# One-hot comparisons in bf16, and four buffers for the first dispatch's normalised rows

## The chip, the cores and the metric

The kernel runs on one core of a Trainium2 chip, as one program. The metric is device time in microseconds (us) from the start to the end of one execution, on that core. An engine's own instruction times are given in us or ns. Engine names are those of the profile: PE is the matrix engine (TensorE), PEld its weight loads, DVE the vector engine, ACT the scalar engine, POOL is GpSimd, SP the queue that issues most DMAs.

## The reference, cut to what matters

The program is a stack of eight residual blocks over `x` of 8 batches x 512 rows x 256 columns: attention and feed-forward by turns. Two of the feed-forward blocks (layers 0 and 2) are mixtures of experts: each of the 4096 rows picks two of eight experts, and the change touches only the code that sorts the rows by expert. For layer 0 the reference is, in essence:

```python
gates = softmax(xf @ gate_w)                  # xf: 4096 rows x 256, normalised
topw, topi = top_k(gates, 2)
topw = topw / sum(topw)
h = einsum('td,edh->teh', xf, w1) + b1        # all experts; only two count
h = gelu(_ln(h, ln1_g, ln1_b))
y = einsum('teh,ehd->ted', h, w2) + b2
out = einsum('ted,te->td', y, combine)        # combine: topw at the chosen two
out = _ln(out + xf, ln_g, ln_b)
```

Layer 2 has the same shape, with a hidden width of 1024, no normalisation inside and the weights from a softmax of the two top logits.

## The kernel before

The stages run one after the other: attention, mixture 0, attention, feed-forward, window attention, mixture 2, attention, feed-forward. A mixture is a `dispatch` stage (L835 to L1104) followed by an expert stage. The expert stage works on 71 tiles (`NTILES`) of 128 rows; each tile belongs to one expert. It fetches its rows with indirect DMAs from the DRAM tensor `rows_in` (`k.zs`), by the row numbers in `k.src`, which the dispatch computes last. No fetch can start before the dispatch has ended.

The dispatch has three parts.

First part, per batch `b` of 512 rows: ACT normalises four tiles into `z[b % Z]` (`normalise`, L958 to L966, the activation is L964), SP stores the buffer to `rows_in` (L903), PE transposes it (`turn`, L920), ACT copies the transposed rows out of PSUM (`copy`, L971), PE computes the eight logits of each row (`logits`, L928). ACT's order is written out by hand: normalise 0 and 1, then for each batch copy `b` and normalise `b + 2`. `Z` is 2, so from `b` = 2 on `normalise(b)` waits until the store of batch `b - 2` has landed (`act.wait_ge(stored[b % 2], ...)`). PE's order is turn 0, and then for each batch turn `b + 1` and logits `b`. Both buffers lie in `work`, a tile whose space later holds the one-hot tiles of the third part. SP's order in the first dispatch is: gate weights, post_b, store 0, the four expert constants (L1575; one is 2048 KB, one 1024 KB, both broadcast to all partitions), and then stores 1 to 7. In the first dispatch POOL also adds `post_b` to each batch of `x` when it has been normalised (L995).

Second part, on DVE alone with three short matmuls of PE between: `select` (L1018 to L1029) picks the two experts of each row, for one half of the tiles after logits 3, for the other after logits 7. Then come prefix sums over tiles and rows (L1037 to L1081), which give each of the 64 row groups (two choices x 32 tiles) its `slot` (place inside a tile, 0 to 127) and its `tile_of` (0 to 70). Every step waits for the one before (`then`).

Third part, eight chunks (`CHUNKS`) of eight row groups (`NJ`), with two buffers each: DVE compares a row of 71 tile numbers with `tile_of` (L1086, 8 x 71 = 568 results per partition, bf16 out), and a row of 128 slot numbers with `slot` (L1088, 8 x 128 = 1024 results, bf16 out). All inputs are float32. One input is a row read again for each group, the other is one element read 71 or 128 times. POOL multiplies the tile one-hot by the group number (L1000), ACT by the row number (L985), and PE multiplies one-hots and names (L951), so that the row numbers appear sorted. DVE's next tile comparison waits for the matmuls two chunks back. After the last chunk DVE computes `k.owner` (L1092 to L1095), and `k.src` and `k.dst` (L1098 to L1104).

Of the kernel before, what the change touches and what calls it, by code (L numbers as in the profile page):

```python
# [16 lines left out]
BF16 = mybir.dt.bfloat16  # L17
I32 = mybir.dt.int32
U32 = mybir.dt.uint32
ALU = mybir.AluOpType  # L20
# [3 lines left out]
P = 128  # L24
NB, SEQ, D = 8, 512, 256
TPB = SEQ // P
# [811 lines left out]
def dispatch(nc, k, L):  # L838
# [12 lines left out]
    with ctx:  # L851
# [4 lines left out]
        Z = 2  # L856
# [11 lines left out]
        z = [work[:, s * (TPB * D):(s + 1) * (TPB * D)] for s in range(Z)]  # L868
# [6 lines left out]
        code = sb(nm + "code", [P, NT])  # L875
        top = [sb(f"{nm}top{j}", [P, NT]) for j in range(TOPK)]
        gap, den = sb(nm + "gap", [P, NT]), sb(nm + "den", [P, NT])
        rank, turn_of, slot, tile_of = (sb(nm + n, [P, TOPK * NT]) for n in ("rank", "turn", "slot", "tile"))
# [11 lines left out]
        stored = [sem(f"{nm}stored{s}") for s in range(2)]  # L890
# [4 lines left out]
        with nc.Block() as block:  # L895
            @block.sync
            def _(sp):
                sp.dma_start(gate[:, :, :], k.a[f"L{L}_gate"]).then_inc(w_in, 16)
                if L == 0:
                    sp.dma_start(post_b[:, :], k.a["L0_ffn_ln_b"].partition_broadcast(P)).then_inc(post_in, 16)  # L900
                for b in range(NB):
                    sp.wait_ge(z_done, b + 1)
                    sp.dma_start(k.zs[P + b * SEQ:P + (b + 1) * SEQ, :].rearrange("(t p) d -> p t d", p=P),  # L903
                                 z[b % Z].rearrange("p (t d) -> p t d", t=TPB)).then_inc(stored[b % 2], 16)
                    if b == 0:
                        load_expert_constants(sp, k, L)
                    k.late(sp, b)
                for s in range(2):
                    sp.wait_ge(stored[s], 16 * NB // 2)
                sp.wait_ge(k.zeroed, 16)  # L910
# [46 lines left out]
            def _(act):  # L957
                def normalise(b):  # L958
                    wait_pos(act, zT_ps, b - Z + 1)
                    if b >= Z:  # L960
                        act.wait_ge(stored[b % 2], 16 * (b // 2))
                    for t in range(TPB):
                        n = b * TPB + t
                        o = act.activation(z[b % Z][:, t * D:(t + 1) * D], k.xt(n), ACT.Identity,  # L964
                                           bias=shift[:, n:n + 1], scale=k.rstd[:, n:n + 1])
                    o.then_inc(z_done, 1)  # L966
# [36 lines left out]
            def _(dve):  # L1003
# [29 lines left out]
                dve.sem_inc(centred, 1)  # L1033
                for h in range(2):
                    select(h)
# [19 lines left out]
                for s in range(2):  # L1055
                    dve.wait_ge(stored[s], 16 * NB // 2)
# [9 lines left out]
                then(dve.scalar_tensor_tensor(slot[:, :], turn_of[:, :], -float(P), rank[:, :], ALU.mult, ALU.add))  # L1066
# [14 lines left out]
                then(dve.tensor_tensor(tile_of[:, :], tile_of[:, :], turn_of[:, :], ALU.add))  # L1081

                for c in range(CHUNKS):
                    s, own = c % 2, slice(c * NJ, (c + 1) * NJ)
                    wait_pos(dve, ids_ps, c - 1)
                    dve.tensor_tensor(at_tile[s][:, :, :], k.cst[:, None, C_J:C_J + NTILES].to_broadcast([P, NJ, NTILES]),  # L1086
                                      tile_of[:, own, None].to_broadcast([P, NJ, NTILES]), ALU.is_equal).then_inc(hot_done, 1)
                    dve.tensor_tensor(at_slot[s][:, :, :], k.cst[:, None, C_I:C_I + P].to_broadcast([P, NJ, P]),  # L1088
                                      slot[:, own, None].to_broadcast([P, NJ, P]), ALU.is_equal).then_inc(slot_done, 1)
# [1448 lines left out]
```

## Time and profile before

| what | us |
|---|---|
| runs of the kernel before | 2286.05, 2288.46, 2291.26 (median 2288.46) |
| profiled execution, device time | 2285.1 |
| its span, first to last instruction | 2283.3 |
| PE busy | 1963.4 (86%) |
| DVE busy | 1310.2 (57%) |
| ACT busy | 941.4 (41%) |
| POOL busy | 593.6 (26%) |
| first dispatch, from DVE's shift (L1032) to `k.dst` (L1104) | 216.7 to 303.6 |
| second dispatch, the same | 1268.6 to 1351.8 |
| mean granted TensorE clock | 0.919 |

The busy shares are means over stages with different limits. Inside the two dispatches the shares are quite other than over the span, so the trace has to be read there, by stretches of time. A duration in the trace covers also the time in which an instruction, already issued, waits for something that is no semaphore.

### The profile page before, as it was taken

To read this page: it belongs to the slowest core of one execution; us is meant where nothing else is said; L and a number is where in the kernel's file an instruction comes from. 1 tells how busy PE (TensorE), PEld (TensorE's weight loads), DVE (VectorE), ACT (ScalarE), POOL (GpSimd) and SP (SyncE) were. 2 spreads that over 40 slices of the span, in tenths; PEclk is the share of its full clock that TensorE was granted. 3 is DMA by queue.
4 is the path that set the end of the run, shared out by engine and by line. 5 is a ranking of instruction groups with operands and counts; after the bars stand their busy time and mean duration, and the time that the engine had idled before them with its cause. 6 is when DMAs were issued, how large, how long until landed. Compare 5 with 4: busy or idle time off the path is not lost. (4 is left out here: it accounts for less than half of the span.)

```text
span 2283.3 us, 37863 instructions
## 1 busy us (share of the span) xinstructions
PE 1963.4 (86%) x11930; PEld 1465.4 (64%) x11931; DVE 1310.2 (57%) x2973; ACT 941.4 (41%) x2050; POOL 593.6 (26%) x582
## 2 busy tenths in 40 slices
PE   6998569999848887999989739999999995998687
PEld 3665536666525553666666729999999983665355
DVE  5885456666558887787655162222222215887987
ACT  3444324444336543333222413333333323553787
POOL 1122246666424431011000032222222221321000
PEclk9999579999959998999989559999999997999899
DMA  7001211111141104000000611111111114100001
GB/s 268 1 1 56 77 49 63 61 64 60 53 162 56 56 1 162 0 1 0 0 15 5 240 33 33 37 34 37 34 37 37 37 31 157 40 20 1 10 28 38
DMA packets 71122, 119.54 MB, mean 52 GB/s; under 512 B 13648, under 2 KB 54736, under 8 KB 67952
## 3 DMA queue, kind: packets, MB, share of 16 engines
q1 hardware_dynamic: 55760, 78.76, 9.9%
q0 software_dynamic: 13680, 37.37, 5.2%
q10 hardware_dynamic: 1584, 2.13, 0.3%
q8 instruction: 58, 0.95, 0.2%
q14 instruction: 40, 0.33, 0.0%
HBM read 86.90 MB, written 31.33 MB: 52 GB/s over the span
## 5 line engine op out<-in xcount | busy, mean ns | idle before, releaser
L1421 ACT ACTIVATE e_hT<-psum,x_bt 128x128 f32<-128x128 f32 x568 | 154.6, 383 | 336.4 <-PE psum L1384 331.7
L1384 PEld LDWEIGHTS psum<-e_xT,e_w 128*128 128x128 f32 x2272 | 268.3, 194 | 8.4 <-ACT e_xT L1414 4.9
L268 POOL TENSOR_TENSOR rstd<-lnt,half 128x4 f32<-128x4 f32 (+1 forms) x72 | 73.3, 1018 | 769.6 <-DVE lnt L262 769.6
L1384 PE MATMUL psum<-e_xT,e_w 128*128 128x128 f32 x2272 | 268.9, 277 | 4.2 <-ACT e_xT L1414 4.2
L1393 PE MATMUL psum<-m_w,e_hT 128*128 x1136 | 256.8, 379 | 0.0
L1393 PEld LDWEIGHTS psum<-m_w,e_hT 128*128 128x128 f32 x1136 | 210.4, 190 | 25.7
L1442 DVE COPY e_w<-m_w 128x2048 f32 x71 | 87.1, 1227 | 234.4 <-PE psum L1384 230.0
L724 DVE TENSOR_REDUCE a_mx<-psum 128x8 f32<-128x512 f32 x192 | 123.2, 684 | 84.0 <-PE psum L515 83.4
L1241 ACT ACTIVATE e_hT<-psum,x_bt,x_gt 128x128 f32<-128x128 f32 x284 | 106.9, 457 | 142.1 <-PE psum L1208 142.1
L1325 POOL DMA_INDIRECT rows_out<-e_y,dst x106 | 106.0, 1000 | 205.7 <-DVE e_y L1452 175.0
L1317 POOL DMA_INDIRECT e_x<-rows_in,src x142 | 142.3, 1002 | 56.8 <-issue 35.2
L640 ACT ACTIVATE a_pT<-psum 128x512 f32<-128x512 f32 x192 | 103.8, 592 | 102.4 <-PE psum L565 102.4
L1218 PE MATMUL psum<-m_w,e_hT 128*128 x568 | 140.4, 390 | 4.0 <-ACT e_hT L1241 3.6
L1199 PE MATMUL psum<-m_w,e_xT 128*128 x284 | 138.2, 609 | 1.4 <-issue 0.6
L1841 PE MATMUL psum<-f_w,f_q 128*128 128x256 f32 x512 | 121.9, 384 | 14.9 <-DVE f_q L1728 14.9
L1841 PEld LDWEIGHTS psum<-f_w,f_q 128*128 128x128 f32 x512 | 97.3, 191 | 55.0 <-issue 30.7
L727 DVE TENSOR_TENSOR a_pr<-psum,a_mx 128x512 f32<-128x512 f32 x192 | 122.9, 682 | 0.7
L1828 PE MATMUL psum<-f_zT,f_w 128*128 128x512 f32 x256 | 121.7, 601 | 0.9 <-DVE f_q L1725 0.9
L1218 PEld LDWEIGHTS psum<-m_w,e_hT 128*128 128x128 f32 x568 | 102.3, 190 | 21.2 <-issue 5.5
L541 PE MATMUL psum<-att_wo,a_oT 128*128 128x256 f32 x384 | 101.4, 387 | 16.5 <-DVE x_res L739 16.5
L487 PE MATMUL psum<-a_zT,att_wq 128*128 128x512 f32 x192 | 103.4, 665 | 7.3 <-ACT a_qT L617 5.2
L244 DVE BATCH_NORM_STATS2 stats<-x_res 128x6 f32<-128x256 f32 (+1 forms) x256 | 98.8, 419 | 12.2 <-PEq L203 8.5
(282 smaller groups left out, 3588.2 us busy)
## 6 DMA issues: line engine op xcount, KB each, us to landing
m_w<-in_L_ffn_w SPq DMA_DIRECT2D x16, 1024.0 KB, 9.3
m_w<-in_L_ffn_w SPq DMA_DIRECT2D x16, 512.0 KB, 12.7
rows_in<-r_work SPq DMA_DIRECT2D x16, 512.0 KB, 5.4
m_w<-rows_out SPq DMA_DIRECT2D x16, 512.0 KB, 5.9
a_ar_g<-rows_out SPq DMA_DIRECT2D x16, 512.0 KB, 5.0
x_res<-in_x SPq DMA_DIRECT2D x8, 512.0 KB, 7.1
m_w<-rows_in SPq DMA_DIRECT2D x8, 512.0 KB, 3.9
out_x<-x_res SPq DMA_DIRECT2D x8, 512.0 KB, 3.0
```

Source lines behind the costliest of these rows:

```text
L724: dve.tensor_reduce(mx[g][:, :], wide[g], AX.X, ALU.max).then_inc(s_max, 1)
L727: dve.tensor_tensor(pr[t % 2][:, g * W:(g + 1) * W].rearrange("p (h l) -> p h l", h=HPC), wide[g], mx[g][:, :, None].to_broadcast([P, HPC, ...
L1199: mm = pe.matmul(h_b[s][:, c * 512:(c + 1) * 512], xT[s][:, kk, :], w1[:, bass.ds(e * (DC * F) + (kk * F + c * 512), 512)], start=(kk == 0 ...
L1218: mm = pe.matmul(y_b[:, 0:D], hT[s][:, f, :], w2[:, bass.ds(e * (FC * D) + f * D, D)], start=(f == 0), stop=(f == FC - 1))
L1241: g = act.activation(hT[s][:, f, :], hT_b[:, f, :], ACT.Gelu, bias=bt[:, col], scale=gt[:, col] if norm else 1.0)
L1317: pool.indirect_dma_start(out=xin[j % 2][:, :], out_offset=None, in_=k.zs[:, :], in_offset=bass.IndirectOffsetOnAxis(ap=k.src[:, j:j + 1], ...
L1325: pool.indirect_dma_start(out=k.ys[:, :], out_offset=bass.IndirectOffsetOnAxis(ap=k.dst[:, j:j + 1], axis=0), in_=y[j % 2][:, :], in_offse ...
L1384: mm = pe.matmul(h_b[s][:, f, :], w1[:, kk, f * P:(f + 1) * P], xT[s][:, kk, :], start=(kk == 0), stop=(kk == DC - 1))
L1393: mm = pe.matmul(y_b[s][:, 0:D], hT[s][:, f, :], k.w2[:, bass.ds(e * (FC * D) + f * D, D)], start=(f == 0), stop=(f == FC - 1))
L1421: g = act.activation(hT[s][:, f, :], h_b[s][:, f, :], ACT.Gelu, bias=bt[:, bass.ds(e * FC + f, 1)])
L1828: mm = pe.matmul(hb[f % HS][:, :], w1[:, kk, f * P:(f + 1) * P], zT[s][:, kk, :], start=(kk == 0), stop=(kk == DC - 1))
L1841: mm = pe.matmul(yb[t % 2][:, 0:D], q[s][:, g, t * P:(t + 1) * P], w2[:, g, :], start=(g == 0), stop=(g == FC - 1))
```

## The change

The two comparisons read bf16 on both sides. Two new tiles, `slots16` and `tiles16`, hold the slot numbers and the tile numbers as bf16; DVE copies them from the float32 constants before `select`. The step that computed `slot` writes bf16 `slot16`, and the step that computed `tile_of` writes its last result to bf16 `tile16`. All these numbers are whole and at most 127, so bf16 holds them exactly. This holds in both dispatches. In the first dispatch alone `Z` is 4: two more buffers of 1024 words each lie beside `work`, there are four semaphores `stored`, and `normalise(b)` waits for the store of batch `b - 4` and for the transpose of batch `b - 4`. The order of ACT, PE and SP stays.

```diff
--- before.py
+++ after.py
@@ -853,7 +853,7 @@
         shift = sb(nm + "shift", [P, NT])
         if L == 0:
             post_b, post_in = sb(nm + "post_b", [P, D]), sem(nm + "post_in")
-        Z = 2
+        Z = 4 if L == 0 else 2
         work = sb(nm + "work", [P, 4 * DC * SEQ])
         taken = [0]
 
@@ -865,7 +865,9 @@
             part = work[:, at:at + words]
             return part.bitcast(BF16) if dtype == BF16 else part
 
-        z = [work[:, s * (TPB * D):(s + 1) * (TPB * D)] for s in range(Z)]
+        z = [work[:, s * (TPB * D):(s + 1) * (TPB * D)] for s in range(2)]
+        if L == 0:
+            z += [sb(f"{nm}z{s}", [P, TPB * D])[:, :] for s in range(2)]
         zT = [work[:, (2 + s) * DC * SEQ:(3 + s) * DC * SEQ].rearrange("p (c q) -> p c q", c=DC) for s in range(2)]
         lgt, eq, rest = (sb(nm + n, [P, NT, E]) for n in ("lgt", "eq", "rest"))
         chosen = k.zero[:, :].rearrange("p (t e) -> p t e", t=NT)
@@ -873,9 +875,11 @@
         old = {c: k.att_w[c][:, :, :].rearrange("p c d -> p (c d)") for c in "qkvo"}
         hot, prod = (old[c].rearrange("p (j t e) -> p j t e", j=TOPK, t=NT) for c in "vo")
         code = sb(nm + "code", [P, NT])
+        slots16, tiles16 = sb(nm + "slots16", [P, P], BF16), sb(nm + "tiles16", [P, NTILES], BF16)
+        slot16, tile16 = (sb(nm + n, [P, TOPK * NT], BF16) for n in ("slot16", "tile16"))
         top = [sb(f"{nm}top{j}", [P, NT]) for j in range(TOPK)]
         gap, den = sb(nm + "gap", [P, NT]), sb(nm + "den", [P, NT])
-        rank, turn_of, slot, tile_of = (sb(nm + n, [P, TOPK * NT]) for n in ("rank", "turn", "slot", "tile"))
+        rank, turn_of, tile_of = (sb(nm + n, [P, TOPK * NT]) for n in ("rank", "turn", "tile"))
         cnt = [sb(f"{nm}cnt{j}", [P, E]) for j in range(3)]
         at_slot = [old[c].bitcast(BF16).rearrange("p (i q) -> p i q", i=NJ) for c in "qk"]
         at_tile = [late(NJ * NTILES, BF16).rearrange("p (i t) -> p i t", i=NJ) for s in range(2)]
@@ -887,7 +891,7 @@
         bank = [ps(f"{nm}b{s}", [P, DC, SEQ]) for s in range(2)]
         lg = [ps(f"{nm}lg{h}", [P, 512]) for h in range(2)]
         pp, idb = ps(nm + "pp", [P, 512]), ps(nm + "ids", [P, 512])
-        stored = [sem(f"{nm}stored{s}") for s in range(2)]
+        stored = [sem(f"{nm}stored{s}") for s in range(Z)]
         (w_in, centred, z_done, zT_ps, zT_copied, lg_ps, lg_read, v, chosen_done, place_ps, gap_done, gap_exp,
          hot_done, slot_done, hi_done, lo_done, ids_ps) = (
             sem(nm + c) for c in ("w_in", "centred", "z_done", "zT_ps", "zT_copied", "lg_ps", "lg_read", "v",
@@ -901,12 +905,12 @@
                 for b in range(NB):
                     sp.wait_ge(z_done, b + 1)
                     sp.dma_start(k.zs[P + b * SEQ:P + (b + 1) * SEQ, :].rearrange("(t p) d -> p t d", p=P),
-                                 z[b % Z].rearrange("p (t d) -> p t d", t=TPB)).then_inc(stored[b % 2], 16)
+                                 z[b % Z].rearrange("p (t d) -> p t d", t=TPB)).then_inc(stored[b % Z], 16)
                     if b == 0:
                         load_expert_constants(sp, k, L)
                     k.late(sp, b)
-                for s in range(2):
-                    sp.wait_ge(stored[s], 16 * NB // 2)
+                for s in range(Z):
+                    sp.wait_ge(stored[s], 16 * NB // Z)
                 sp.wait_ge(k.zeroed, 16)
 
             @block.tensor
@@ -958,7 +962,7 @@
                 def normalise(b):
                     wait_pos(act, zT_ps, b - Z + 1)
                     if b >= Z:
-                        act.wait_ge(stored[b % 2], 16 * (b // 2))
+                        act.wait_ge(stored[b % Z], 16 * (b // Z))
                     for t in range(TPB):
                         n = b * TPB + t
                         o = act.activation(z[b % Z][:, t * D:(t + 1) * D], k.xt(n), ACT.Identity,
@@ -1031,6 +1035,8 @@
 
                 then(dve.scalar_tensor_tensor(shift[:, :], k.mean[:, :], -1.0, k.rstd[:, :], ALU.mult, ALU.mult))
                 dve.sem_inc(centred, 1)
+                then(dve.tensor_copy(slots16[:, :], k.cst[:, C_I:C_I + P]))
+                then(dve.tensor_copy(tiles16[:, :], k.cst[:, C_J:C_J + NTILES]))
                 for h in range(2):
                     select(h)
                 dve.wait_ge(k.zeroed, 16)
@@ -1052,8 +1058,8 @@
                 then(dve.tensor_tensor(k.wt[1][:, :], k.wt[1][:, :], k.wt[0][:, :], ALU.mult))
 
                 dve.wait_ge(place_ps, 1)
-                for s in range(2):
-                    dve.wait_ge(stored[s], 16 * NB // 2)
+                for s in range(Z):
+                    dve.wait_ge(stored[s], 16 * NB // Z)
                 both = lambda t: t[:, :, :, :].rearrange("p j t e -> p j (t e)")
                 each = lambda t: t[:, :, :, :].rearrange("p j t e -> p (j t) e")
                 tiles = cnt[0]
@@ -1063,7 +1069,7 @@
                 then(dve.tensor_scalar(turn_of[:, :], rank[:, :], 1.0 / P, -(0.5 - 0.5 / P), ALU.mult, ALU.add))
                 then(dve.tensor_scalar(turn_of[:, :], turn_of[:, :], MAGIC, None, ALU.add))
                 then(dve.tensor_scalar(turn_of[:, :], turn_of[:, :], MAGIC, None, ALU.subtract))
-                then(dve.scalar_tensor_tensor(slot[:, :], turn_of[:, :], -float(P), rank[:, :], ALU.mult, ALU.add))
+                then(dve.scalar_tensor_tensor(slot16[:, :], turn_of[:, :], -float(P), rank[:, :], ALU.mult, ALU.add))
 
                 then(dve.tensor_scalar(tiles[:, :], tiles[:, :], P - 1.0, 1.0 / P, ALU.add, ALU.mult))
                 then(dve.tensor_scalar(tiles[:, :], tiles[:, :], -(0.5 - 0.5 / P), MAGIC, ALU.add, ALU.add))
@@ -1078,15 +1084,15 @@
                 then(dve.tensor_tensor(start[:, :], end[:, :], tiles[:, :], ALU.subtract))
                 then(dve.tensor_tensor(each(prod), each(hot), start[:, None, :].to_broadcast([P, TOPK * NT, E]), ALU.mult))
                 then(dve.tensor_reduce(tile_of[:, :], each(prod), AX.X, ALU.add))
-                then(dve.tensor_tensor(tile_of[:, :], tile_of[:, :], turn_of[:, :], ALU.add))
+                then(dve.tensor_tensor(tile16[:, :], tile_of[:, :], turn_of[:, :], ALU.add))
 
                 for c in range(CHUNKS):
                     s, own = c % 2, slice(c * NJ, (c + 1) * NJ)
                     wait_pos(dve, ids_ps, c - 1)
-                    dve.tensor_tensor(at_tile[s][:, :, :], k.cst[:, None, C_J:C_J + NTILES].to_broadcast([P, NJ, NTILES]),
-                                      tile_of[:, own, None].to_broadcast([P, NJ, NTILES]), ALU.is_equal).then_inc(hot_done, 1)
-                    dve.tensor_tensor(at_slot[s][:, :, :], k.cst[:, None, C_I:C_I + P].to_broadcast([P, NJ, P]),
-                                      slot[:, own, None].to_broadcast([P, NJ, P]), ALU.is_equal).then_inc(slot_done, 1)
+                    dve.tensor_tensor(at_tile[s][:, :, :], tiles16[:, None, :].to_broadcast([P, NJ, NTILES]),
+                                      tile16[:, own, None].to_broadcast([P, NJ, NTILES]), ALU.is_equal).then_inc(hot_done, 1)
+                    dve.tensor_tensor(at_slot[s][:, :, :], slots16[:, None, :].to_broadcast([P, NJ, P]),
+                                      slot16[:, own, None].to_broadcast([P, NJ, P]), ALU.is_equal).then_inc(slot_done, 1)
 
                 wide = lambda t: t.to_broadcast([1, NTILES, E])
                 then(dve.tensor_tensor(ended[:, :, :], wide(k.cst[0:1, C_J:C_J + NTILES, None]), wide(end[0:1, None, :]),
```

## Rows read from the trace of the kernel before

**Rows 1.** The page: span of the profiled execution.
```profile
span 2283.3 us, 37863 instructions
```
**Rows 2.** Busy time by stretch: dispatch 1 (first four), dispatch 2 (last two).
```profile
core 0: us, PE busy (x) PEld busy (x) DVE busy (x) ACT busy (x) POOL busy (x), PEclk, DMA share, GB/s
...
219.10:228.70 9.60, 9.48 (x56) 8.87 (x56) 0.00 (x0) 5.93 (x10) 6.98 (x3) 0.68 0.98 331
228.70:234.60 5.90, 0.00 (x0) 0.00 (x0) 0.00 (x0) 2.10 (x5) 0.00 (x0) 0.50 0.78 278
234.60:263.30 28.70, 28.65 (x136) 28.55 (x136) 6.98 (x12) 13.73 (x22) 11.78 (x5) 0.50 0.28 92
...
278.30:301.00 22.70, 8.47 (x62) 6.48 (x63) 22.63 (x19) 6.16 (x8) 16.42 (x8) 0.50 0.00 1
...
1280.40:1282.80 2.40, 0.03 (x2) 0.01 (x1) 0.00 (x0) 2.14 (x5) 0.00 (x0) 0.50 1.00 393
1282.80:1311.50 28.70, 28.64 (x136) 28.55 (x136) 3.48 (x12) 14.02 (x22) 0.00 (x0) 0.50 0.88 352
```
**Rows 3.** Timeline around batch 3: start, duration, engine, line; idle before and its releaser.
```profile
225.87 2.80 PE L928 MATMUL psum<-r_gate,r_work 128*128 128x8 f32 x16
...
232.50 2.07 ACT L964 ACTIVATE r_work<-x_res,r_shift,rstd 128x256 f32<-128x256 f32 x4 [6.70 <-DMA rows_in<-r_work]
...
234.62 1.97 PE L920 MATMUL psum<-cst,r_work 128*128 128x128 f32 x8 [5.95 <-ACT r_work L964]
...
239.66 1.95 PE L920 MATMUL psum<-cst,r_work 128*128 128x128 f32 x8
```
**Rows 4.** DMA issues, 221.5 to 223 us: KB each, us from issue to landing.
```profile
x_b<-in_L_ffn_b SPq DMA_DIRECT2D x1, 2048.0 KB, 9.9
rows_in<-r_work SPq DMA_DIRECT2D x1, 512.0 KB, 10.4
```
**Rows 5.** Busy time in two single microseconds: PEclk is the seventh column from the left.
```profile
225.00:226.00 1.00, 1.00 (x10) 0.95 (x10) 0.00 (x0) 0.80 (x1) 1.00 (x2) 1.00 1.05 422
...
227.00:228.00 1.00, 1.00 (x6) 1.00 (x6) 0.00 (x0) 0.00 (x0) 0.70 (x1) 0.50 1.12 442
```
**Rows 6.** Timeline of the chunk loop, dispatch 1: its start, one period, its end.
```profile
278.35 0.75 DVE L1086 TENSOR_TENSOR r_work<-cst,r_tile 128x568 bf16<-128x568 f32 x1
...
280.16 1.68 DVE L1086 TENSOR_TENSOR r_work<-cst,r_tile 128x568 bf16<-128x568 f32 x1
...
281.76 1.21 DVE L1088 TENSOR_TENSOR att_wk<-cst,r_slot 128x1024 bf16<-128x1024 f32 x1
...
281.92 2.05 POOL L1000 TENSOR_TENSOR r_work<-r_work,cst 128x568 bf16<-128x568 bf16 x1 [0.68 <-DVE r_work L1086]
282.89 1.67 DVE L1086 TENSOR_TENSOR r_work<-cst,r_tile 128x568 bf16<-128x568 f32 x1
...
299.29 1.67 DVE L1092 TENSOR_TENSOR r_work<-cst,r_cnt 1x568 f32<-1x568 f32 x1
```
**Rows 7.** Groups by line and shape, DVE: count, busy us, mean ns.
```profile
L1442 DVE COPY e_w<-m_w 128x2048 f32 x71 | 87.1, 1227 | 234.4 <-PE psum L1384 230.0 <-issue 3.0 <-PEq L895 1.4
L1725 DVE SCALAR_TENSOR_TENSOR f_q<-f_u,f_c,psum 128x512 f32<-128x512 f32 x64 | 47.5, 742 | 0.0
L757 DVE SCALAR_TENSOR_TENSOR delta<-a_part,cst,delta 128x512 bf16<-128x512 bf16 x2 | 1.5, 751 | 0.1
```
**Rows 8.** POOL beside DVE outside the dispatches: two timeline rows, one group by line.
```profile
1010.12 0.69 DVE L1720 TENSOR_TENSOR f_u<-f_u,f_near 128x512 f32<-128x512 f32 x1
...
1010.42 2.60 POOL L1655 TENSOR_TENSOR x_res<-x_res,f_b 128x1024 f32 x1
...
L438 POOL TENSOR_TENSOR x_res<-x_res,att_bo 128x1024 f32<-128x1024 f32 x24 | 56.7, 2363 | 1.2 <-ACT a_z L604 1.2
```
**Rows 9.** Timeline: DVE's first step after the logits; PE's first after the dispatch.
```profile
244.85 0.29 DVE L1018 COPY r_lgt<-psum 128x128 f32<-128x128 f32 x1 [27.96 <-PE psum L928]
...
309.62 0.66 PE L1190 MATMUL psum<-cst,e_x 128*128 128x128 f32 x2 [8.08 <-DMA e_x<-rows_in,src]
```

## The prediction

> **What bounds the kernel now.** I read the page first, then busy time by stretches inside the two dispatches, then the timeline of those stretches. The profiled execution has a span of 2283.3 us and a device time of 2285.1 us, so 1.8 us lie outside the span [rows 1]. The dispatches take some 87 and 83 us of it. They stand between two barriers: PE's first matmul of the experts waits for rows that are fetched by numbers which the dispatch computes last [rows 9], and no other stage runs beside it. So whatever shortens the chain inside a dispatch shortens the whole time by as much, and nothing outside a dispatch is touched.
>
> The chain inside has three limits in turn, and the reader is to look at which engine's column fills each stretch [rows 2].
>
> In the first part it is PE: 28.65 of 28.70 us busy from 234.6 to 263.3. Before it, from 228.7 to 234.6, PE does nothing for 5.90 us. The timeline says why [rows 3]: turn 3 waited 5.95 us for ACT's normalise 3, and this waited 6.70 us for a DMA. The DMA is the store of batch 1, issued at 222.03 behind the expert constants; it took 10.4 us to land where the constant of 2048 KB ahead of it took 9.9 [rows 4].
>
> In the second part it is DVE alone, step after step.
>
> In the third part DVE is busy 22.63 of 22.70 us [rows 2], but that figure misleads. One period is from 280.16 to 282.89, 2.73 us [rows 6]. The tile comparison takes 0.75 us when it runs first (278.35) and 1.68 in the loop: issued at 280.16 it ends at 281.84, and POOL's multiplication of the same chunk had been running. In the next period POOL ends at 281.92 + 2.05 = 283.97, and the comparison that was issued at 282.89 ends at 282.89 + 1.67 = 284.56, 0.59 us later. So the tile comparison stands still until POOL is through, and then runs for about 0.6 us. POOL in turn starts 0.08 us after the comparison's end. The period is POOL 2.05 + comparison 0.60 + 0.08 = 2.73. The slot comparison (1.21 us) is not a term of this sum, unless POOL stands still for it, which is the question below.
>
> **Part 1: four buffers in the first dispatch.** Removed is the wait of normalise 3 for store 1. Followed step by step with the measured durations: ACT ends normalise 2 at about 224.2, copy 1 (1.0 us) at 225.2, normalise 3 (2.07) at 227.3. PE ends logits 1 at 225.87 + 2.80 = 228.67 [rows 3], so turn 3 then waits for PE itself and starts at about 228.7 in place of 234.62. This is the whole 5.9 us gap [rows 2].
>
> What is late next? Normalise 4 waits for store 0, long landed. Normalise 5 waits for store 1, which lands at 222.03 + 10.4 = 232.4 [rows 4]. PE needs normalise 5 only for turn 5. A turn and its logits take 239.66 - 234.62 = 5.04 us [rows 3], so turn 5 is due at 228.7 + 10.1 = 238.8 and normalise 5, 2.07 us long, could start as late as 236.7. The cover is 4.3 us. Stores 2 and 3 are now issued sooner, beside store 1; in the kernel before such a store had 512 KB, and at the 331 GB/s of that stretch [rows 2] the two are 1.05 MB or 3.2 us of traffic, so even if all of it got ahead of store 1 the cover holds by 1.1 us. Normalise 6 and 7 wait for stores 2 and 3, and are due 5 and 10 us later still. From turn 3 on PE was gapless before and stays so; everything to the end of logits 7 moves 5.9 us forward.
>
> TensorE's clock could change this. It was at its upper level (1.00, 2.4 GHz) at 225 and at its lower (0.50, 1.2 GHz) from 227 on, while PE was busy throughout [rows 5]. After that it stayed at 0.50 through 28.7 us without a gap, in both dispatches [rows 2]. Since turn 3 falls after the drop in the new order too, I take 0.50 for the same 136 matmuls, and 28.7 us again.
>
> Added in this part are two waits on DVE ahead of the rank computation and two on SP. No row prices a wait whose semaphore is already up. Bounded from below by nothing, from above by the 0.1 us or so between dependent DVE steps, they cost 0 to 0.2 us; I take 0.1. SP's lie beside DVE's 40 us chain. The added copies of constants are hidden: DVE sits idle for 27.96 us before its first step after the logits [rows 9], and would still for 22; the two copies are each no longer than the 0.29 us of that 128-column copy. In the second dispatch the same idle time covers them. Without that cover they would cost 0.6 us each time.
>
> Sum of part 1: -5.9 + 0.1 = -5.8 us.
>
> **Part 2: comparisons in bf16.** The count of elements and the access pattern stay. One input has single elements repeated 71 or 128 times in the innermost dimension. Nothing in the trace is a two-tensor DVE operation in bf16 with such an input, so I bound it. The nearest row is a two-tensor operation with 512 bf16 elements in and out: 751 ns, against 742 ns for the same kind of instruction in float32 [rows 7]. Its bf16 gives nothing. The other end is the float32 copy with one source, 2048 elements in 1.227 us [rows 7], that is two elements per 1.2 ns: DVE can take two at a time, and if a comparison in bf16 could, it would halve. The first row is nearer, for it has two tensor sources as the comparison has. Cost of part 2 taken: 0 for all 32 comparisons. The steps that now write bf16 `slot16` and `tile16` have 64 elements and stay as long.
>
> The Trainium skill has two rules here. VectorE: DVE Perf Modes, section on the perf-mode tier table, says that a bf16 tensor_tensor between SBUF tiles runs at twice the rate of float32; by that alone the change would gain what rival A gives. Vector Engine (DVE) Microarchitecture Reference, section 5.1, says that the doubled mode wants a step of one in every operand, and reports that with one element read again and again as one source of a two-source operation it ran at single rate. By that the sum is the -5.8 us above. No run here shows either yet.
>
> **Forecast.** 2285.1 - 5.8 = 2279.3 us for a profiled execution like this one. The profiled execution lay 3.4 us below the median of the runs, so against the median: 2288.5 - 5.8 = 2282.7 us, 0.25% faster.
>
> **The rivals.**
>
> A. The comparisons halve. From 1.21 us for 1024 and 0.75 for 568 elements [rows 6] one element costs 1.01 ns and the rest is 0.18 us. Halved, the slot comparison takes 0.69 and the running part of the tile comparison 0.60 - 0.29 = 0.31. What that brings depends on whether POOL stands still for the slot comparison. For it: in the feed-forward stage a POOL addition of 1024 elements took 2.60 us where 2.363 is the mean, and a two-source DVE operation that began before it ended 0.39 us after POOL's start [rows 8]. The loop has the same order: slot comparison at 281.76, POOL at 281.92. And 568 elements at POOL's rate (2.36 us for 1024) would be 1.3 us, not 2.05. So POOL probably starts its work when the slot comparison ends (282.97) and takes 1.00 from there. Then the period falls by 0.52 from the slot comparison and 0.29 from the tile comparison, 0.81. Per dispatch: seven periods 5.7, the first comparison 0.3, the last slot comparison 0.5 (what follows it, at 299.29, stays float32): 6.5, twice 13.0. Time: 2282.7 - 13.0 = 2269.7. If POOL needs its 2.05 us anyway, only the tile comparison counts: 16 x 0.29 = 4.6, and 2278.1. Against all of A: the bf16 row of 751 ns.
>
> B. The gap is filled but the gain is lost, because store 1 comes late for normalise 5 as well, or ACT's normalise 3 finds another holder of its buffer. This needs store 1 to land after 236.7 + 5.9 us. Time 2288.5, no change. The 4.3 us of cover speak against it, and that the DMA engines have room after 234.6, where their share is 0.28 [rows 2].
>
> C. Slower: repeated bf16 elements cost DVE two cycles each in place of one. The place is the chunk loop, all 16 chunks. The slot comparison grows by 1024 x 1.01 ns = 1.03 us, and POOL stands still for it; the tile comparison grows by 0.57. The period grows by 1.60, sixteen times 25.6 us: 2282.7 + 25.6 = 2308.3. It decides from 0.36 us per chunk on (5.8 / 16), where the gain of part 1 is eaten, and shows as slower by over 0.2% from 0.65 us per chunk on. Against it: bf16 at step one cost 9 ns more in 742 [rows 7]. For it: only that no row has bf16 with repeated elements.
>
> **How the numbers follow.** Forecast 0.78, A 0.14 (0.10 with POOL released, 0.04 without), B 0.05, C 0.03. The forecast's own range is -5 to -6.5 us, with the two medians' own scatter of about 3 us (the three runs spread over 5.2): 2279 to 2287. To reach 8 in 10 I take in B above and A's weaker form below: 2277 to 2289. A's stronger form and C stay outside, 0.13 together. What a measurement of this kernel can tell from no change is about 0.2%, 4.6 us. The forecast's 5.8 is just above that: of its 0.78 I give 0.53 to faster by over 0.2% and 0.25 to within. With A on the one side, B within and C slower: faster 0.67, same 0.30, slower 0.03.
>
> **What would show it right or wrong.** In the profile after: turn 3 of the first dispatch (L920) starts at 228.7 with no idle time before it, and no ACT normalise waits longer than 1 us for a store; logits 7 end at about 257.4. The second dispatch's first part stays as it is, its 2.40 us gap [rows 2] too. L1086 and L1088 keep 0.75 / 1.67 and 1.21 us, and L1000 keeps 2.05; a slot comparison of 0.7 us would be rival A, and L1000 then tells by 1.5 or 2.05 us which form. A slot comparison above 1.5 us is C. The clock in 234 to 257 at 0.50; were it at 1.00 for part of it, I would be wrong on the fast side.

## The result and the profile after

The changed kernel took 2274.85 us (median of 6 runs, 2272.96 to 2278.99), the kernel before, measured beside it, 2287.26 (6 runs, 2281.55 to 2291.26). The ratio is 0.9949, with a 95% interval of 0.9933 to 0.9965: 11.7 us faster, 8 to 15 by the interval. Forecast were 5.8 us and 2282.7 us, with a range of 2277 to 2289. The time lies below the range. A second comparison of the same two kernels (run `again` below) gave 0.9967, 0.9956 to 0.9978, so 7.5 us, 5 to 10. The intervals overlap from 8 to 10 us. All ratios here leave out slow executions, of which there were two, both of the run `z3` (2321.13 and 2717.28 us).

The page's first line, and then the busy time by stretch (width, busy time and count of PE, PEld, DVE, ACT, POOL, then PEclk, DMA share, GB/s). The first two stretches are the first part of dispatch 1, the third its chunk loop.

```profile
span 2273.2 us, 37869 instructions
```

```profile
216.80:225.90 9.10, 8.99 (x57) 8.62 (x58) 0.00 (x0) 9.01 (x16) 7.22 (x4) 0.69 0.98 316
225.90:254.40 28.50, 28.50 (x137) 28.40 (x136) 7.55 (x12) 12.66 (x21) 11.46 (x5) 0.50 0.46 161
269.40:291.20 21.80, 7.89 (x56) 5.89 (x56) 21.77 (x18) 6.15 (x8) 16.14 (x8) 0.50 0.00 1
```

The 5.90 us in which PE did nothing [rows 2] are gone: the 136 matmuls follow the first 56 at once, and take 28.5 us at the lower clock, where the kernel before took 28.65. The timeline shows the batches (start, duration, instruction, and in brackets the idle time before):

```profile
219.75 2.06 ACT L968 ACTIVATE r_z<-x_res,r_shift,rstd 128x256 f32<-128x256 f32 x4
...
222.30 1.07 PE L924 MATMUL psum<-cst,r_z 128*128 128x128 f32 x8
...
223.20 2.71 PE L932 MATMUL psum<-r_gate,r_work 128*128 128x8 f32 x16
...
225.77 1.95 PE L924 MATMUL psum<-cst,r_z 128*128 128x128 f32 x8
...
232.41 2.07 ACT L968 ACTIVATE r_work<-x_res,r_shift,rstd 128x256 f32<-128x256 f32 x4 [3.63 <-DMA rows_in<-r_work]
...
235.79 1.95 PE L924 MATMUL psum<-cst,r_work 128*128 128x128 f32 x8
```

Turn 3 (225.77) has no idle time before it; it comes 11.36 us after the dispatch's first DVE step at 214.41, where the kernel before had it at 234.62 - 216.70 = 17.92 [rows 3]. ACT's wait did not vanish, it moved two batches on: normalise 5 waits 3.63 us for store 1. Normalise 5 ends at 234.48 and turn 5 starts without idle time at 235.79. Store 1 now took longer, from issue to landing:

```profile
rows_in<-r_work SPq DMA_DIRECT2D x1, 512.0 KB, 12.6
```

against 10.4 us [rows 4]. The chunk loop did not change at all. First one period of it, as in rows 6, and then the two comparisons by shape over both dispatches (count, busy us, mean ns):

```profile
272.87 1.21 DVE L1094 TENSOR_TENSOR att_wk<-r_slots,r_slot 128x1024 bf16<-128x1024 bf16 x1
...
273.03 2.05 POOL L1004 TENSOR_TENSOR r_work<-r_work,cst 128x568 bf16<-128x568 bf16 x1 [0.68 <-DVE r_work L1092]
274.00 1.68 DVE L1092 TENSOR_TENSOR r_work<-r_tiles,r_tile 128x568 bf16<-128x568 bf16 x1
```

```profile
L1092 DVE TENSOR_TENSOR r_work<-r_tiles,r_tile 128x568 bf16<-128x568 bf16 x16 | 24.9, 1559 | 0.1
L1094 DVE TENSOR_TENSOR att_wq<-r_slots,r_slot 128x1024 bf16<-128x1024 bf16 x8 | 9.7, 1213 | 0.0
```

Inputs in bf16 on both sides, and 1.21 us as in float32 [rows 6].

Where do the 10.1 us between the two profiled spans lie? The table cuts each span at the start of the first DVE step of a dispatch (shift) and at the start of its last (`k.dst`). "Its loop" is part of dispatch 1: from the start of the first comparison to the start of the step behind the last one. The table has all profiled executions, one of each kernel; the experiments are explained below. "Logits 0" is the duration of the first batch's 16 logit matmuls on PE, which tells the clock: 1.85 to 2.04 where it rose to the upper level, 3.42 at the lower.

| kernel | to dispatch 1 | dispatch 1 | its loop | between | dispatch 2 | rest | span | logits 0 |
|---|---|---|---|---|---|---|---|---|
| before | 216.7 | 86.7 | 20.9 | 965.2 | 82.9 | 931.8 | 2283.3 | 2.04 |
| null | 216.1 | 87.3 | 20.9 | 960.5 | 82.8 | 932.2 | 2278.9 | 1.85 |
| bf16 | 215.0 | 87.8 | 20.9 | 963.6 | 82.9 | 927.1 | 2276.4 | 1.87 |
| after | 214.4 | 80.1 | 20.9 | 964.4 | 83.1 | 931.2 | 2273.2 | 1.85 |
| again | 218.6 | 83.2 | 20.9 | 963.4 | 83.3 | 932.0 | 2280.5 | 3.42 |
| z4 | 218.7 | 80.1 | 20.9 | 961.3 | 82.8 | 931.4 | 2274.3 | 1.95 |
| z3 | 218.7 | 83.2 | 20.9 | 963.6 | 82.8 | 928.1 | 2276.4 | 3.42 |
| const_late | 215.7 | 83.2 | 20.9 | 965.1 | 80.4 | 931.4 | 2275.7 | 3.42 |
| slot_step | 218.2 | 75.8 | 16.7 | 961.7 | 78.8 | 927.8 | 2262.3 | 1.85 |
| both_step | 214.9 | 78.7 | 16.2 | 963.2 | 78.0 | 933.5 | 2268.3 | 3.42 |
| names_step | 214.7 | 79.9 | 16.6 | 965.8 | 79.4 | 932.3 | 2271.9 | 3.42 |
| best | 215.3 | 75.6 | 16.2 | 962.1 | 75.6 | 928.6 | 2257.2 | 1.89 |
| best2 | 215.7 | 75.8 | 16.7 | 962.1 | 76.3 | 931.3 | 2261.2 | 1.98 |
| best3 | 219.1 | 79.8 | 16.6 | 963.5 | 76.8 | 931.6 | 2270.9 | 3.42 |

From before to after: 2.3 us ahead of dispatch 1, 6.6 in it, 0.8 between, -0.2 in dispatch 2, 0.6 in the rest. Only the 6.6 are in code that the change touches.

### The profile page after: what moved, and what is told of

The parts are those of the page before. It is cut to its first block and busy times, and to the rows that moved or that the text cites. A ratio compares the mean times of both kernels' runs of the same rounds, so it can differ in the third digit from the quotient of the medians.

```text
span 2273.2 us, 37869 instructions
## 1 busy us (share of the span) xinstructions
PE 1962.6 (86%) x11930; PEld 1464.5 (64%) x11931; DVE 1311.3 (58%) x2977; ACT 941.6 (41%) x2050; POOL 592.4 (26%) x582
## 5 line engine op out<-in xcount | busy, mean ns | idle before, releaser
L541 PE MATMUL psum<-att_wo,a_oT 128*128 128x256 f32 x384 | 100.9, 385 | 16.4 <-DVE x_res L739 16.4
```

## The experiments

Two theories were open. **Theory S** (scatter): the change gives some 6.6 us, all in dispatch 1, and the rest of the 11.7 is scatter of stretches that no edit touches. **Theory H** (hidden effect): something systematic outside that stretch gives another 5 us. The first, second, third and fourth run below (`again`, `z4`, `bf16`, `null`) are to tell them apart. Runs measured together share their runs of the kernel before: its median was 2284.61 us beside these four, 2284.85 beside `const_late`, `slot_step`, `both_step` and `best`, and 2283.91 beside `z3`, `names_step`, `best2` and `best3`. A gain in us is the ratio times that median.

### again: the change once more

> The changed kernel once more. Theory S (scatter): its first dispatch gives 6.6 us, and the other 5 us of the 11.7 us that were measured are scatter of the stretches that no edit touches, so this time it comes out between 5 and 9 us below the kernel before. Theory H (hidden effect): something systematic outside the first dispatch gives another 5 us; then it comes out 10 us or more below again.

Measured: 2275.72 us (8 runs, 2274.01 to 2282.27), ratio 0.9967 (0.9956 to 0.9978), 7.5 us. That is the middle of the 5 to 9 us of theory S. Its profile showed something that had not been expected: dispatch 1 took 83.2 us, not 80.1, without a gap on PE and without a wait of ACT for a store. Its first logits:

```profile
224.77 3.42 PE L932 MATMUL psum<-r_gate,r_work 128*128 128x8 f32 x16
```

The same instructions took 1.85 us in the profile of after. The granted clock over eight microseconds from the start of PE's work (PEclk is third from the right), first `again`, then `after`:

```profile
221.00:225.00 4.00, 3.91 (x18) 3.54 (x19) 0.00 (x0) 3.91 (x8) 2.83 (x2) 0.50 0.90 269
225.00:229.00 4.00, 4.00 (x20) 4.00 (x21) 0.00 (x0) 3.84 (x7) 4.00 (x2) 0.50 1.04 383
```

```profile
217.00:221.00 4.00, 3.91 (x21) 3.54 (x20) 0.00 (x0) 3.91 (x8) 2.32 (x2) 0.56 0.96 294
221.00:225.00 4.00, 4.00 (x34) 4.00 (x34) 0.00 (x0) 4.00 (x8) 4.00 (x3) 0.87 1.00 321
```

In one execution the clock rises to its upper level (2.4 GHz) for a few microseconds, in the other it stays at the lower (1.2 GHz), with the same work before and under it. Why is not shown: PE had stood 6.33 us before this work in `again` and 6.32 in `after`.

### z4: the four buffers alone

```diff
-        Z = 2
+        Z = 4 if L == 0 else 2
...
-        stored = [sem(f"{nm}stored{s}") for s in range(2)]
+        stored = [sem(f"{nm}stored{s}") for s in range(Z)]
```

The comparisons keep their float32 inputs.

> Only the four buffers of the first dispatch, comparisons in float32 as before. Theory S: 5.5 to 7 us below the kernel before, within 2 us of the whole change. Theory H, if the hidden part belongs to the buffers: 10 to 13 us below. If it belongs to bf16: 5.5 to 7 us below, and the whole change 5 us faster than this.

Measured: 2275.18 us, ratio 0.9967 (0.9953 to 0.9980), 7.5 us. This equals the whole change in `again`. It is 0.5 us more than theory S expected, with an interval of 4.6 to 10.7 us. Dispatch 1 takes 80.1 us.

### bf16: the comparisons alone

```diff
-                                      slot[:, own, None].to_broadcast([P, NJ, P]), ALU.is_equal)
+                                      slot16[:, own, None].to_broadcast([P, NJ, P]), ALU.is_equal)
```

> Only the bf16 comparisons, two buffers as before. Theory S: no difference, within 2 us of the kernel before; both comparison lines keep 1.21 and 0.75 or 1.67 us. Theory H, if the hidden part belongs to bf16: 5 us below the kernel before.

Measured: 2283.28 us, ratio 0.9996 (0.9988 to 1.0005), 0.9 us with an interval over zero. The loop keeps 20.9 us (20.94 in either profile). The bf16 half of the change does nothing that can be told from zero.

### null: the kernel before, a second time

> The kernel before, unchanged, built and loaded a second time. Theory S: its median can differ from that of the first by 2 to 4 us, by loading alone, and its early stretch (the first 56 us, where transfers land) differs most. Theory H: within 1 us of the kernel before.

Measured: 2283.39 us, ratio 0.9997 (0.9987 to 1.0007). So two builds of one kernel agree within 1.2 us when their medians come from 12 and 28 runs, and no 2 to 4 us by loading were seen. Here theory H had expected the right thing and theory S had not. Single executions scatter much more: the profiled ones of before and null differ by 4.4 us in span, 4.7 of it in the stretch between the dispatches. So the scatter is there, but it is from execution to execution, and largest between the dispatches and not in the early stretch. Theory H stays unlikely for another reason: `z4` and `again` both gave 7.5 us. The upper ends of their intervals, 10.7 and 10.0 us, just reach the 10 us that it needs, so it is not ruled out.

### const_late: the same gap closed from the other side

```diff
-                    if b == 0:
+                    if b == NB - 1:
                         load_expert_constants(sp, k, L)
```

> The kernel before with one move: SP issues the expert constants after store 7 in place of after store 0, in both dispatches; two buffers, float32 comparisons. If the queue of constants ahead of store 1 is the cause of the gap, the stores land in about 3 to 4 us, PE's 5.95 us gap in the first dispatch closes without any new buffer, and the time falls by 5.5 to 7 us, like the four buffers; in the second dispatch the weight loads are still ahead of the stores, so at most 1 to 2 us of its 2.4 us gap go. If the cause were the buffers themselves (two are too few even for undisturbed stores), the gap stays at 2 us or more.

Measured: 2274.50 us, ratio 0.9955 (0.9942 to 0.9968), 10.3 us. The point lies above that of the four buffers, but the intervals overlap. With two buffers as before, PE has no gap in dispatch 1 (83.2 us; the clock stayed at its lower level in this execution), and in dispatch 2 the stage shrank from 82.9 to 80.4 us, the whole gap of 2.40 us [rows 2]. Normalise 3 of the first dispatch and turn 3 of the second:

```profile
224.47 2.07 ACT L964 ACTIVATE r_work<-x_res,r_shift,rstd 128x256 f32<-128x256 f32 x4
...
1275.59 1.97 PE L920 MATMUL psum<-cst,r_work 128*128 128x128 f32 x8
```

No idle time stands before either. A lower clock makes PE later and could hide a gap in dispatch 1, but normalise 3 ended at 226.54, 10.9 us after the dispatch's first step at 215.68, and turn 3 of `after` started 11.36 us after it with the clock risen early. So no gap would be left there either (an estimate from the two profiles). The stores landed in 2.9 us (the median of eight), less than the 3 to 4 us expected. So two buffers are enough once the stores are not held up; the 3 MB of constants ahead of store 1 were what held it, and the 1 MB of them in dispatch 2 as well.

### z3: is a third buffer enough?

Against z4; the waits for the stores are counted to fit.

```diff
-        Z = 4 if L == 0 else 2
+        Z = 3 if L == 0 else 2
```

> Three buffers in the first dispatch in place of four, float32 comparisons. By the reasoning on what is late next: normalise 4 now waits for store 1, which lands some 18 us after the dispatch's first step, so turn 4 starts near 20.5 us after it where PE would be ready at 16.4: a gap of about 4 us remains and the gain over two buffers is about 2 to 3 us in place of 6.6. The rival: any third buffer is enough, and it equals the four.

Measured: 2279.84 us (the median of all eleven; 2278.99 without the two that the ratio leaves out), ratio 0.9984 (0.9975 to 0.9993), 3.7 us. That is half of the four buffers' gain and a little over the 2 to 3 us expected. Its interval and those of `again` (from 0.9956 to 0.9978) and `z4` (from 0.9953 to 0.9980) touch, so that three buffers give less than four is likely and not certain. Its profiled execution is one at the lower clock. ACT's normalise 4 waited there for store 1:

```profile
235.44 2.07 ACT L966 ACTIVATE r_work<-x_res,r_shift,rstd 128x256 f32<-128x256 f32 x4 [4.24 <-DMA rows_in<-r_work]
...
238.22 1.95 PE L922 MATMUL psum<-cst,r_work 128*128 128x128 f32 x8
```

Turn 4 has no idle time before it, so this wait cost PE nothing. With the clock risen early turn 4 would be due 16.4 us after the dispatch's first step (in `after` it started at 230.78) and would find normalise 4 ended 18.8 us after it: an estimated gap of 2.4 us. No profile shows that case.

### slot_step: the slot comparison with a step of one in all operands

The diffs of this and the next two runs are cut to the lines that change a layout or how it is read. This one is against the changed kernel and the next two each against the run before it; declarations and the waits for the spread-out constants are left out, in both_step also the turned tile comparison and ACT's line.

```diff
-        at_slot = [... .rearrange("p (i q) -> p i q", i=NJ) for c in "qk"]
+        at_slot = [... .rearrange("p (q i) -> p q i", i=NJ) for c in "qk"]
-                        mm = pe.matmul(idb[:, 0:2 * NTILES], at_slot[s][:, i, :],
+                        mm = pe.matmul(idb[:, 0:2 * NTILES], at_slot[s][:, :, i],
+                act.activation(slots16[:, :, :], k.cst[:, C_I:C_I + P, None].to_broadcast([P, P, NJ]), ACT.Copy)
-                    dve.tensor_tensor(at_slot[s], slots16[:, None, :].to_broadcast([P, NJ, P]),
-                                      slot16[:, own, None].to_broadcast([P, NJ, P]), ALU.is_equal)
+                    dve.tensor_tensor(at_slot[s], slots16[:, :, :],
+                                      slot16[:, None, own].to_broadcast([P, P, NJ]), ALU.is_equal)
```

> The changed kernel, but the slot comparison's result and both its inputs have the row group innermost (a step of one in all three; the constant is spread out once by ACT); the tile comparison stays with a repeated element. If the repeated element keeps bf16 at single rate, the slot comparison falls from 1.21 to about 0.7 us. If then POOL's multiplication had been standing still for it, POOL's 2.05 us fall to about 1.5 and the time by 0.52 us for each of 16 chunks, 8 us below the changed kernel. If POOL needs 2.05 us by itself, the time stays. If bf16 at a step of one is no faster either, both durations stay.

Measured: 2269.67 us, ratio 0.9935 (0.9920 to 0.9949). One period of its loop:

```profile
276.12 0.68 DVE L1100 TENSOR_TENSOR att_wk<-r_work,r_slot 128x1024 bf16<-128x1024 bf16 x1
...
276.27 1.52 POOL L1010 TENSOR_TENSOR r_work<-r_work,cst 128x568 bf16<-128x568 bf16 x1 [0.68 <-DVE r_work L1098]
276.85 1.55 DVE L1098 TENSOR_TENSOR r_work<-r_tiles,r_tile 128x568 bf16<-128x568 bf16 x1
```

The slot comparison fell by 0.53 us and POOL's multiplication, of which nothing was edited, by 0.53 as well. The loop fell from 20.94 to 16.67 us in either dispatch, 8.5 together, where 8 were expected; by the ratios, 0.9935 against 0.9967, it is 7.3 us. This is the price that rival A put on the slot comparison (0.52 us a chunk), got by the layout and the type together and not by the type alone; float32 in the new layout was not run.

### both_step: the tile comparison too

```diff
-        at_tile = [late(NJ * NTILES, BF16).rearrange("p (i t) -> p i t", i=NJ) for s in range(2)]
+        at_tile = [late(NJ * NTILES, BF16).rearrange("p (t i) -> p t i", i=NJ) for s in range(2)]
-                    pool.tensor_tensor(names[s][:, :, 0, :], at_tile[s][:, :, :], hi, ALU.mult)
+                    pool.tensor_tensor(names[s][:, :, 0, :], at_tile[s].rearrange("p t i -> p i t"), hi, ALU.mult)
```

> As the last one, the tile comparison too with the row group innermost; POOL and ACT then read its result with a step of eight elements. If pairing works for both, the tile comparison runs for about 0.3 us in place of 0.6 after POOL ends, and the time is 4 to 5 us below that of the last kernel, some 12 us below the changed kernel. If POOL or ACT are slowed by the stepped read, POOL's line shows it and eats this.

Measured: 2271.13 us, ratio 0.9938 (0.9924 to 0.9952): nothing gained on slot_step, where 4 to 5 us were expected. ACT reads its result in the same steps as POOL. The groups by line and shape:

```profile
L1012 POOL TENSOR_TENSOR r_work<-r_work,cst 128x568 bf16<-128x568 bf16 x16 | 28.6, 1785 | 91.1 <-DVE r_work L1099 91.1
L997 ACT ACTIVATE r_work<-r_work,cst 128x568 bf16<-128x568 bf16 x16 | 21.6, 1351 | 23.4 <-DVE r_work L1099 23.4
```

The comparison itself now takes 0.45 us when it runs first, against 0.75. But POOL, reading in steps of eight, takes 1.79 us in place of 1.52, ACT 1.35 in place of 0.77. The period is 2.18 us against 2.20: what the comparison gained went to POOL's 0.27 us more. The expectation had named this as what would eat the gain.

### names_step: POOL and ACT in steps of one, PE in steps of eight

```diff
-        names = [... .rearrange("p (i a t) -> p i a t", i=NJ, a=2) for s in range(2)]
+        names = [... .rearrange("p (a t i) -> p a t i", i=NJ, a=2) for s in range(2)]
-                                       names[s][:, i, :, :].rearrange("p a t -> p (a t)"),
+                                       names[s][:, :, :, i].rearrange("p a t -> p (a t)"),
```

> As both comparisons with the row group innermost, and now the names too, so that POOL and ACT read and write in steps of one and only PE's moving operand is read in steps of eight elements. If the stepped read was what took POOL from 1.52 to 1.79 us, it returns to about 1.5 and the period falls from 2.18 to about 1.9 us: 4 us below that kernel. If PE's matmul is slowed by its own stepped read, its 0.33 us grows, and from 0.24 us per matmul more on PE would set the period.

Measured: 2272.77 us, ratio 0.9948 (0.9935 to 0.9961). The 4 us expected below both_step did not come. PE became the bound:

```profile
275.09 2.24 PE L957 MATMUL psum<-r_work,att_wq 128*128 128x142 bf16 x8 [8.24 <-POOL r_work L1012]
...
277.38 0.46 DVE L1099 TENSOR_TENSOR r_work<-r_work,r_tile 128x568 bf16<-128x568 bf16 x1 [1.42 <-PE psum L957]
```

Eight matmuls took 2.24 us where both_step had 1.17 and the kernel before 1.13, and the tile comparison stood 1.42 us until the matmuls of two chunks back were through. POOL took 1.66 us, not the 1.5 expected, with a step of one in what it reads and writes; its group numbers were read in another order too, and why it stayed slower is open. Reading PE's stationary operand in the same steps (slot_step) had cost it nothing to speak of: 1.16 us for eight.

### best, best2, best3: put together

Each adds the late constants (the edit of const_late) to one of the last three kernels: best to both_step, best2 to slot_step, best3 to names_step.

> The last kernel, with the expert constants issued after store 7. If the causes add up: the first dispatch has no gap and no dependence on when store 1 lands, the second loses up to 1 to 2 us of its gap: 1 to 3 us below the last kernel, 20 us below the kernel before.

> Slot comparison with the row group innermost, four buffers in the first dispatch, and the expert constants after store 7: 8.5 us from the comparison, 7 to 8 from the first dispatch, 1 to 3 from the second: 2284.8 - 18 = 2267.

> The names-innermost kernel with the expert constants after store 7: 4 us below the last one if POOL returns to 1.5 us, so about 2263, 22 us below the kernel before.

Measured: best 2266.87 us, ratio 0.9925 (0.9910 to 0.9940); best2 2265.18 us, 0.9924 (0.9911 to 0.9937); best3 2266.70 us, 0.9932 (0.9919 to 0.9945). The intervals overlap, so which of the three is first is not settled. Best2 is the simplest and is 17.4 us faster than the kernel before, some 10 us faster than the changed kernel; 18 had been expected of it, and 20 of best, which gave 17.1. Dispatch 2 falls from 83.1 (after) to 76.3 and 75.6 us. Best3 was expected at 2263 and its loop, 16.6 us, was bound by PE as in names_step.

## Why the prediction was right or wrong

**Part 2, the comparisons: right, by a row that was partly luck.** They were costed at nothing, by the 751 ns row [rows 7]; they gave 0.9 us with an interval over zero. The slot comparison stayed at 1.21 us. But the 751 ns row is a scalar_tensor_tensor with a step of one in its tensors, and it was read as saying that bf16 gives two-source operations nothing. slot_step shows that a bf16 comparison with a step of one does gain: 1024 elements in 0.68 us. What kept the changed kernel's comparisons slow is the repeated element, and no row of before had one in bf16. Vector Engine (DVE) Microarchitecture Reference, section 5.1, in the Trainium skill had said that a source with one element read again and again keeps single rate; the trace agrees with 1.21 us for 1024 bf16 elements, and with 0.68 us once the same comparison had a step of one. The rule of the Trainium skill in VectorE: DVE Perf Modes, section on the perf-mode tier table, that bf16 doubles the rate of a tensor_tensor, held nearly for the slot comparison in slot_step (0.68 us, with the fixed part of the instruction in it) and not in the changed kernel (1.21 us). The sub-step of rival A that was called probable, that POOL stands still for the slot comparison, is shown by POOL's 2.05 going to 1.52 us. The Trainium skill's page SBUF — State Buffer, section on who interferes with whom, says that a DVE instruction with two SBUF inputs and a GpSimd instruction that reads SBUF exclude each other. The trace agrees in both orders: POOL's multiplication took 2.05 us behind a comparison of 1.21 us and 1.52 behind one of 0.68, and DVE's tile comparison took 1.55 to 1.68 us behind POOL's multiplication and 0.75 when it ran first. Rival B's late store came (the 3.63 us below) and cost PE nothing. Rival C had no part: a repeated bf16 element costs what a repeated float32 element costs.

**Part 1, the mechanism: right.** The gap closed, turn 3 lost its idle time, nothing new appeared on PE, the clock in the later stretch stayed at 0.50, the second dispatch kept its gap. One sign did not come: no normalise was to wait longer than 1 us for a store, and normalise 5 waited 3.63. The cover of normalise 5 was put at 4.3 us, and at 1.1 us if the stores issued sooner got ahead of store 1. The cover did shrink to that: the store took 12.6 us, and 1.1 us was left (PE's first weight load of turn 5 at 235.58, normalise 5 ended at 234.48). That the stores issued sooner did it is not shown apart from scatter: store 1 took 12.6 and 12.8 us in `after` and `z4`, and 10.4, 11.0 and 11.6 in the three profiles with two buffers.

**Part 1, the size: mis-sized.** The term was -5.9, and the profile has 86.7 - 80.1 = 6.6. The step that failed is that PE "ends logits 1 at 225.87 + 2.80 = 228.67", where turn 3 was to start: it took the time of PE's earlier work over from the trace of before, 11.97 us after the dispatch's first step. In `after` logits 1 ended 11.50 us after it, and turn 3 started at 11.36. Turn 2 started 0.35 us earlier there, counted from the first step (7.89 in place of 8.24), logits 1 ended a further 0.12 us earlier against it, and a turn without an idle PE starts 0.14 us before the logits' end.

The same edit removes a wait in front of all this: normalise 2 had waited 0.68 us for store 0. The prediction moved normalise 2 forward for ACT (to 224.2) and not for PE. In the profile of before PE itself was busy with logits 0 until 8.24 (they took 2.04 us, 1.85 in `after`), so there at most 0.14 of the 0.35 us is that wait. In the profile of null logits 0 took 1.85 us as well, PE stood 0.25 us before turn 2, and logits 1 took 3.28 us:

```profile
224.35 1.10 PE L920 MATMUL psum<-cst,r_work 128*128 128x128 f32 x8 [0.25 <-ACT r_work L964]
225.28 3.28 PE L928 MATMUL psum<-r_gate,r_work 128*128 128x8 f32 x16
```

In all five profiles with four buffers and an early clock rise (`after`, `z4`, `slot_step`, `best`, `best2`) turn 3 started at 11.36 or 11.37 us. The 0.1 us for the added waits did not show: turn 3 came 6.56 us earlier and the dispatch's last step 6.60.

One execution is also a narrow base for a gap that ends with a DMA: in the profiles of null and bf16 PE stood 6.12 and 6.80 us before turn 3, and 0.25 and 0.16 before turn 2, not 5.95. Against the mean of the three profiles with two buffers, 87.3 us, the gain is 7.2 us when the clock rises early. When it doesn't, it would be 4.1 (87.3 against the 83.2 of again), if the kernel before takes its 87.3 us there too, which no profile shows. Which share of the executions has which clock was not measured.

**The time itself: outside the range, in about half by its base.** The other term that failed is what the -5.8 was taken from. The sum started from 2288.46 us, the median of three runs; the 28 runs beside the first four experiments had 2284.61. That is 3.9 of the 7.9 us by which 2274.85 falls under the forecast (2.2 under the range's lower end). The prediction saw that the profiled execution lay 3.4 us under that median, and carried its sum to the higher one without asking which of the two was the odd one. Of the other 4.0 us, 1.7 lie between the 5.8 forecast and the 7.5 of two comparisons, whose intervals take in 5.8, and 2.3 came with the first comparison alone. The range's allowance for the medians' own scatter, about 3 us, was too small: the stretches that no edit touched ran over 4.7 us ahead of dispatch 1, 5.3 between the dispatches and 6.4 after them (the table), and the twelve runs of null from 2279.41 to 2289.42.

**The first comparison's 11.7 us** stay partly open. That they are scatter beyond 7.5 is what again, z4 and null say together; no profile can show it for the six runs themselves. A larger share of executions with an early clock rise among those six, worth up to 3.1 us (83.2 - 80.1), is a rival that was not tested.

## What to carry to other kernels

When a producer waits for its buffer's store, look first at what is queued ahead of the store. Moving constants that nobody needs before the expert stage (3 MB in one dispatch, 1 MB in the other) closed the gap in both dispatches without a buffer. It was worth 10.3 us, and the buffers 7.5, with intervals that overlap. Here a narrower type paid on DVE only once every operand stepped by one (1.21 us to 0.68); ask of each broadcast which dimension it repeats, and what the new layout costs the engines that read the result. And when one edit removes several waits on one chain, restart the chain from its first removed wait, not from the place where the trace of before had the gap. Before a forecast of 0.25% is set against a time, take the base from many runs: three were off by 3.9 us, more than half of the gain forecast.

## What the runs showed of the hardware

TensorE's granted clock at the start of a stage is not the same in each execution. Of the fourteen profiled executions eight had the first dispatch's logits at the upper level (1.85 to 2.04 us for 16 matmuls) and six at the lower (3.42 us), with the same work before them. It is worth 3.1 us where PE is the bound: dispatch 1 took 80.1 us in `after` and 83.2 in `again`, 75.6 in `best` and 78.7 in `both_step`, with the same loop in each pair. In the second dispatch all fourteen had it at the upper level (1.85 to 2.05 us).

PE reading bf16 in steps of eight elements (16 bytes) took twice as long for the moving operand, 2.24 us for eight matmuls against 1.13 to 1.17, and next to nothing more for the stationary one, 1.16 us. ACT paid 1.35 us in place of 0.77 for the same step in its input, and POOL 1.79 us in place of 1.52.
